# Attention and expert 0 taken in two halves of the batch, the first half ahead; the inverse deviation computed half by half on VectorE

## What is computed

```python
# step 1: autocorrelation attention
Q = layernorm(x) @ Wq + bq;  K = ctx[:, :56] @ Wk + bk;  V = ctx[:, :56] @ Wv + bv     # 16 heads of 8
corr = irfft(rfft(Q) * conj(rfft(K)))          # along the 56 positions
w, idx = top_k(corr.mean(-1), 4)               # 4 best shifts of each batch and head
out = sum_k softmax(w)_k * roll(V, -idx_k)
x = x + tanh(g_xattn) * (out @ Wo + bo)
# step 2: mixture of 8 experts, 2 per token
xf = layernorm(x)
weights = softmax over the two largest of (xf @ Wr + br)
x = x + tanh(g_ffn) * sum_e weights_e * (gelu(xf @ W1[e] + b1[e]) @ W2[e] + b2[e])     # hidden size 512
```

## Time and profile before

| | us |
|---|---|
| median of 3 executions (lowest, highest) | 133.50 (132.34, 134.25) |
| the profiled execution, its own time | 132.46 |
| its span, first to last instruction | 130.2 |
| mean granted clock of TensorE in it | 0.956 of full |
| PE busy | 117.5 (90%) |
| DVE busy | 89.9 (69%) |
| ACT busy | 80.5 (62%) |
| POOL busy | 62.9 (48%) |

### The profile page before, as it was taken

One profiled execution on the slowest core, in us unless ns is written; L12 is line 12 of the kernel. 1 busy time (PEld: TensorE's weight loads), 2 busy tenths in 40 slices (PEclk: granted clock), 3 DMA queues, 4 the chain that ended last, 5 costly groups with the idle time before them and its releaser, 6 DMA issues.

```text
span 130.2 us, 1685 instructions
## 1 busy us (share of the span) xinstructions
PE 117.5 (90%) x575; PEld 94.7 (73%) x575; DVE 89.9 (69%) x175; ACT 80.5 (62%) x107; POOL 62.9 (48%) x50
## 2 busy tenths in 40 slices
PE   6999969998878993959999999999999999999950
PEld 2397555544465891939999999999999999999930
DVE  1583687529386498999679877775775775775991
ACT  3027764401355755928878878878878878878900
POOL 0001460005203999999999999980330330330802
PEclk9999995559999999999999999999999999999998
DMA  3896000000310215400891340030040030000003
GB/s 93 234 406 249 0 0 5 3 0 0 101 60 0 82 79 161 162 6 9 238 337 43 107 146 0 0 141 0 0 141 3 5 141 0 0 0 0 0 0 141
DMA packets 3833, 10.07 MB, mean 77 GB/s; under 512 B 697, under 2 KB 1066, under 8 KB 3826
## 3 DMA queue, kind: packets, MB, share of 16 engines
q1 hardware_dynamic: 3154, 9.43, 21.5%
q10 hardware_dynamic: 672, 0.55, 1.5%
HBM read 9.49 MB, written 0.49 MB: 77 GB/s over the span
## 4 chain that ended last, share of the span: by engine, by line
PE 70%; DVE 14%; ACT 5%; issue 5%; POOL 2%; POOLq 1%; DVEq 0%
PE bank L772 23%; PE bank L799 22%; PE bank L641 7%; PE bank L658 3%; ACT prod L409 3%; POOL cf L329 2%; DVE hidl L617 2%; PE bank L664 2%; ACT hidh L416 2%; DVE prod L496 2%; DVE tw L496 2%; PE bank L718 2%; PE bank L735 1%; DVE qk L261 1%; PE bank L748 1%
## 5 line engine op out<-in xcount | busy, mean ns | idle before, releaser
L617 DVE TENSOR_TENSOR hidl<-prod,hidh 128x896 fp32r<-128x896 f32 (+1 forms) x34 | 45.3, 1339 | 19.8 <-ACT hidh L416 19.8
L409 ACT ACTIVATE prod<-bank,col_sb 128x896 f32<-128x896 f32 (+1 forms) x34 | 32.9, 967 | 14.5 <-PE bank L772 11.8
L323 POOL TENSOR_TENSOR wel<-we_sb,weh 128x512 fp32r<-128x512 f32 x16 | 25.6, 1604 | 20.9 <-issue 19.9
L416 ACT CAST hidh<-prod 128x896 fp32r<-128x896 f32 (+1 forms) x34 | 30.5, 899 | 1.0
L329 POOL TENSOR_TENSOR cf<-cf,kf 128x448 f32<-128x448 f32 x12 | 17.9, 1496 | 26.6 <-DVE kf L604 26.4
L799 PE MATMUL bank<-hidl,weh 128*128 128x448 f32 x64 | 18.5, 368 | 2.2 <-DVE hidl L617 2.2
L772 PE MATMUL bank<-xth,weh 128*128 128x448 f32 x64 | 18.6, 366 | 0.3 <-ACT xth L404 0.3
L772 PE MATMUL bank<-xtl,weh 128*128 128x448 f32 x64 | 18.6, 367 | 0.0
L772 PE MATMUL bank<-xth,wel 128*128 128x448 f32 x64 | 18.5, 365 | 0.0
L799 PE MATMUL bank<-hidh,weh 128*128 128x448 f32 x64 | 18.4, 367 | 0.0
L799 PE MATMUL bank<-hidh,wel 128*128 128x448 f32 x64 | 18.3, 365 | 0.0
(11 more groups left out here) (118 smaller groups left out, 116.7 us busy)
## 6 DMA issues: line engine op xcount, KB each, us to landing
we_sb<-in_w_experts SPq DMA_DIRECT2D x8, 512.0 KB, 5.0
route_b<-route_scratch SPq DMA_DIRECT2D x8, 448.0 KB, 3.6
out<-vf SPq DMA_DIRECT2D x2, 224.0 KB, 1.9
tb<-in_tab_b SPq DMA_DIRECT2D x1, 297.0 KB, 6.3
ta_c<-in_tab_ctx SPq DMA_DIRECT2D x1, 274.8 KB, 4.9
wa_sb<-in_w_attn SPq DMA_DIRECT2D x1, 256.0 KB, 5.7
x_sb<-in_x SPq DMA_DIRECT2D x1, 224.0 KB, 3.8
x_sb<-in_x ACTq DMA_DIRECT2D x1, 224.0 KB, 4.1
```

The costliest lines, as they stand in the source:

```text
L323: gp.tensor_tensor(wel[:, e, k, :], we_sb[:, e % RING, k, :], weh[:, e, k, :].bitcast(F32), ALU.subtract).then_inc(we_split, 1)
L409: act.activation(hid[:, n % 2, halves, :], bank[:, 2 * (n % 2):2 * (n % 2) + 2, 0:TOK][:, halves, :], ACT.Gelu, bias=col_sb[:, P_B1 + n:P_ ...
L416: act.copy(hidh[:, n % SLOTS, halves, :], hid[:, n % 2, halves, :]).then_inc(hid_hi, 1)
L617: ve.tensor_tensor(hidl[:, n % SLOTS, halves, :], hid[:, n % 2, halves, :], hidh[:, n % SLOTS, halves, :].bitcast(F32), ALU.subtract).then ...
```

## The change

- The attention, the second normalisation and expert 0 are done by half: the first half of the batch goes ahead on every engine, the second follows. Each step is a function of the half, and every engine has a list of calls in which first-half steps of a later stage stand ahead of second-half steps of an earlier one. Chunks 0 to 3 are four `hidden` and four `project` for the first half, then the same for the second.
- DVE's inverse deviation is computed per half: the chain of the kernel before, which was run once on 112 x 8 numbers per normalisation, is run twice on 112 x 4. (Both kernels use the seed and the refinement steps on DVE; neither takes a power on GpSimd.)
- The filler matmuls: 7 + 5 at the start instead of 13, none later.
- Logits and their differences take both halves at once, before hidl of chunk 1; DVE's chain of the routes is cut in two by one hidl.
- ACT rather than DVE copies the turned shift weights and both spectra of x, and `take_expert` (7, half) is followed by an addition that DVE does alone.
- POOL: the bias rows are loaded from its queue; xres in two parts, ahead of the centring matrix and only once both first normalisations are over; the rests of experts 0 and 1 in 16 pieces of 128 columns, as soon as ACT has made the rounded part; experts 2 to 7 only once the routes are computed (`route_ok`).
- SP loads experts 5 to 7 between the broadcasts of the routes instead of ahead of them.

```diff
         def _(sp):
-            for e in range(E - 1):
+            for e in range(RING + LEAD_BY_SCALAR):
                 load_expert(e)
...
             for e in range(E):
-                if e == ROUTES:
-                    load_expert(E - 1)
                 if e >= ROUTES:
                     sp.wait_ge(scaled_ok, 2 * (e - ROUTES + 1))
                 sp.dma_start(route_b[:, e % ROUTES, :, :], ...)
+                if e >= 1 and e + RING + LEAD_BY_SCALAR - 1 < E:
+                    load_expert(e + RING + LEAD_BY_SCALAR - 1)
         def _(gp):
+            gp.dma_start(rows_sb[:, :, :], bias_rows).then_inc(in_rows, 16)
+            def rest(e, k):
+                for at in range(0, H, PIECE):
+                    gp.tensor_tensor(wel[:, e, k, at:at + PIECE], ..., ALU.subtract).then_inc(we_split, 1)
...
+            gp.wait_ge(norm_ok, 2)
...
+            residual(0)
+            residual(1)
...
+            for e in range(LEAD_BY_SCALAR):
+                gp.wait_ge(in_we[e], 16)
                 for k in range(2):
...
+                    rest(e, k)
+            gp.wait_ge(route_ok, 1)
+            for e in range(LEAD_BY_SCALAR, E):
+                gp.wait_ge(in_we[e], 16)
+                for k in range(2):
+                    gp.tensor_copy(weh[:, e, k, :], we_sb[:, e % RING, k, :]).then_inc(lead_p, 1)
...
         def _(act):
+            chunk(0, HALF[0])
+            gelu(1, HALF[0])
+            normalise(x2, 1, 1)
+            lead_of_hidden(1, HALF[0])
+            gelu(2, HALF[0])
+            lead_of_tokens(1)
+            lead_of_hidden(2, HALF[0])
+            chunk(3, HALF[0])
+            chunk(0, HALF[1])
+            chunk(1, HALF[1])
+            act.wait_ge(ldif_ok, 1)
+            act.activation(ltanh[:, :, :], ldif[:, :, :], ACT.Tanh, scale=0.5).then_inc(ltanh_ok, 1)
+            chunk(2, HALF[1])
+            chunk(3, HALF[1])
         def _(ve):
+            def variances(times, half):
+                tiles = slice(half * HT, (half + 1) * HT)
...
+                link(ve.tensor_scalar(v, mv[:, tiles, 1], EPS, None, ALU.add))
+                link(ve.tensor_scalar(a.bitcast(I32), v.bitcast(I32), -0.5, GUESS, ALU.mult, ALU.add))
...
         def _(pe):
-            pe.wait_ge(warm_ok, 1)
-            keep_busy(FILL_START, 3)
...
-            keep_busy(FILL_TOP)
...
-            keep_busy(FILL_STEP)
...
-            keep_busy(FILL_NORM)
...
+            hidden(0, HALF[0])
+            hidden(1, HALF[0])
+            logits(1)
+            hidden(2, HALF[0])
+            project(0, HALF[0])
+            tokens_turned(1)
+            hidden(3, HALF[0])
+            project(1, HALF[0])
+            hidden(0, HALF[1])
...
+            hidden(4, BOTH)
+            project(2, HALF[1])
+            turn_routes()
+            hidden(5, BOTH)
+            project(3, HALF[1])
```

More of the change, by code:

```diff
@@ L433, in _ @@
+            chunk(2, HALF[1])
+            chunk(3, HALF[1])
+            for n in range(HC, LAST):
+                chunk(n, BOTH)
+            chunk(LAST, HALF[0])
+            chunk(LAST, HALF[1])
         @block.vector
@@ L492, in _ @@
[L492 to L500 removed]
+                    ve.wait_ge(x2_ok, half + 1)
+                    ve.wait_ge(x_spec, half + 1)
@@ L732, in _, with attention @@
                 mm.then_inc(y_mm, 1)
-            for half in range(2):
+            def attention(half):
                 pe.wait_ge(y_ok, half + 1)
@@ L803, in project @@
-                if n < E * HC - 1:
-                    mm.then_inc(y_expert, 1)
-            hidden(0)
-            hidden(1)
-            for n in range(E * HC):
-                if n + 2 < E * HC:
-                    hidden(n + 2)
-                if n == 3:
-                    turn_routes()
-                project(n)
+                for k, (w, t) in enumerate(operands):
+                    pe.wait_ge(hid_ok if k == 2 else hid_hi, unit(n, last))
+                    for half in range(halves.start, halves.stop):
+                        mm = pe.matmul(bank[:, 6 - 2 * (e % 2) + half, 0:TOK], w_of(w), t[:, slot, half, :],
+                                       start=(c == 0 and k == 0), stop=(c == HC - 1 and k == 2))
@@ new lines, in project @@
+                mm.then_inc(y_expert, 1)
+            pe.wait_ge(warm_ok, 1)
+            keep_busy(FILL_FIRST, 3)
+            pe.wait_ge(dc_ok, 1)
+            pe.wait_ge(in_rows, 16)
+            for half in range(2):
+                open_projection(0, 6, half)
+                open_projection(1, 4, half)
+            keep_busy(FILL_SECOND, 3)
+            context_spectra(0)
+            context_spectra(1)
+            x_spectra(0)
+            pe.wait_ge(in_wa, 16)
+            keys(0)
+            queries(0)
@@ new lines, in _ @@
+            x_spectra(1)
+            keys(1)
+            queries(1)
+            pe.wait_ge(in_tb, 16)
+            head_sums(0)
+            values(0)
+            correlations(0)
+            head_sums(1)
+            weights_turned(0)
+            correlations(1)
+            weight_spectra(0)
+            values(1)
+            repeated(0)
+            weights_turned(1)
+            add_residual(0)
+            weight_spectra(1)
+            output_products(0)
+            repeated(1)
+            attention(0)
```

591 lines of the change are left out of this document (310 added, 281 removed).

## The result

The changed kernel takes 138.17 us (median of 4 executions, 136.80 to 139.24), the kernel before 133.88 beside it (four executions here, 132.34 to 134.29). The ratio is 1.043 with a 95% interval of 1.031 to 1.054: slower, where I had forecast 131.8 us and no measurable change.

What follows compares the result with a forecast made beforehand. Time was taken as the routes' end, plus PE's unbroken expert matmuls behind it, plus whatever breaks that stretch: 49.0 + 73.0 + 7.5 = 129.5 us of span, with 2.26 around it 131.8; range for 8 in 10, 127.8 to 136.0.

Steps and rivals of the forecast that it cites:

- The routes at 49.0: End of the routes, after attention and expert 0: forecast at 49.0 us, between 48.0 and 53, 8.6 us earlier than before.
- I add 0.5 us for the clock and the bias rows: Allowance added to the routes' end of 48.5 us for a lower clock and for bias rows over POOL's queue.
- I get the first product at 13.9: Start of attention: DVE's first-half queries-times-keys product (prod) begins at 13.9 us, 0.3 earlier than before.
- the half clock: Rival: without fillers PE's clock stays at half from 18 us until expert 0 is under way; 138.8 us, chance 10%.
- "about seven" products: In the slow-clock rival: about seven 464- and 512-column products on the path, each 0.8 us more at half clock.
- before had ten us at half clock as well: Argument against the slow-clock rival: the kernel before also ran ten us at half clock, so only the excess counts.
- The halves themselves: Attention by halves: weights-times-values product (tw) at 23.4 us, 5.3 earlier; first gelu at 37.6, 5.6 earlier.
- the second: In attention: the second half's weights-times-values product starts at 27.3 us, after PE's first-half output products.
- The wait that takes the place of the gain: At the take of expert 2's output: DVE waits 8.0 us for POOL, PE stands still 5.3; 7.5 in all.
- the 1.2 that I took: After PE's idle stretch at expert 2: cost of the clock falling, taken as 1.2 us out of 0 to 3.4.
- Behind the routes, 73.0: From the routes to the end, without the new wait: 72.6 us before, 0.6 more for PE, 0.2 less at the end.
- Sum: Whole kernel: 49.0 + 73.0 + 7.5 = 129.5 us of span, with 2.26 around it 131.8 us.

Runs made afterwards that it cites:

- e3: Changed kernel with bias rows loaded from SP's queue and POOL's pairs started at the second normalisation instead of the routes: 133.42 us.
- e6: Changed kernel with all 13 starting fillers ahead of the wait for the bias rows, none behind (13 + 0): 135.90 us.
- e7: Changed kernel with 13 + 0 starting fillers, bias rows from SP's queue and 18 later fillers: 132.52 us, ratio 0.995 to the kernel before.
- e4: Changed kernel with 18 later fillers put into attention and ahead of expert 0: 134.13 us, ratio 1.022 to the kernel before.
- e13: e10 with DVE's first-half xtl ahead of the second half's inverse-deviation chain and 1 filler instead of 4 ahead of expert 0: 124.18 us, ratio 0.940.
- e8: e7 with POOL's additions placed in turns between its pairs: 126.71 us, ratio 0.935 to the kernel before.
- e11: Changed kernel with POOL's additions and pairs in turns, nothing else altered: 131.15 us.
- e9: Kernel before with POOL's pairs of experts 2 to 7 behind the routes and SP's loads of experts 5 to 7 between the broadcasts: 137.63 us, ratio 1.034.
- e10: e8 with five more fillers, 3 ahead of the head sums and 2 ahead of the correlations: 124.95 us, ratio 0.936.
- e1: Changed kernel with its bias rows loaded from SP's queue instead of POOL's: 137.48 us.
- e2: Changed kernel with POOL's pairs of experts 2 to 7 started at the second normalisation instead of at the routes: 134.83 us.

## Why the prediction was wrong, and where it was right

**The routes at 49.0: wrong by 6.6, and this is the step that failed.** "I add 0.5 us for the clock and the bias rows" stood for two terms, and both were mis-sized.

- *Start, "I get the first product at 13.9".* It came at 15.9. I priced the load at "nothing to 1 us" because 5 fillers stand behind it, and took those fillers for cover. They are the cost: PE has nothing left ahead of the wait, and does them after it, in 2.3 us (1.4 in e3). e6 gives 1.8 us back by order alone, e7 2.1. The queue of the load, about which I had argued, is 0.1 to 1.0, by the times at which PE could start on the rows.
- *The half clock.* e4 and e7 need 34.7 and 35.0 us from the first prod to the routes, the changed kernel 39.7: 4.7 to 5.0 us. It costs 1.25 between prod and tw, where steps of PE on the path are few (11.5 against 10.25 in e7), and 3.2 between the first gelu and the routes (13.9 against 10.7), where PE is dense. The rest, 0.3, lies between.

Between the changed kernel and e7 the two are 2.1 and 4.7, all of the 6.9 by which the routes differ (55.62 - 48.75). Taken one at a time, from e6 and from e4, they are 1.8 and 5.0.

I had this outcome as a rival, the half clock, at 138.8 us and 10%, deciding from routes after 53.4. Routes at 55.6 and 138.2 us are nearly its numbers, but in part by luck. It had the clock at half from 18 us until expert 0 without a break, for 5.5 us, and nothing for the start; the clock fell twice, with 10 us at full between, for 4.7, and the start added 2.0. The 5.5 was in the main "about seven" products at 0.8 each, which misreads the rows: 3.22 for four matmuls against 0.95 for two is 0.33 for one and 0.66 for a pair. I set the rival aside because "before had ten us at half clock as well". But those ten us were in the thin steps of attention, where the fall cost the changed kernel 1.25; its second fall is where the matmuls of expert 0 are, and costs 3.2. By the range, 127.8 to 136.0, the outcome had been left out.

**The halves themselves: right, once start and clock are what the steps assumed.** In e7, prod at 13.8 (13.9), tw at 24.0 (23.4), the second at 27.8 (27.3), xtl done at 37.5 (37.2), gelu at 38.1 (37.6), routes at 48.8 (48.5, to which I added the 0.5). The step from prod to tw was 0.75 longer than I had it and that from the first gelu to the routes 0.2 shorter (10.7 against 9.4 + 1.5). That xtl stands behind the second half's chain, and is late for it, e13 shows: 0.8 us, together with three fillers.

**The wait that takes the place of the gain: right, in place and size.** 8.10 against 8.0 for DVE and 5.17 against 5.3 for PE in the changed kernel. Counted from the routes, DVE comes to the take after 24.9 us (24.1) and POOL's addition ends after 32.9 (32.1): both 0.8 later, which cancels in the wait. Behind the routes there are 74.2 to 74.5 us in the halved kernels without the wait and 81.5 to 82.6 in those with the whole of it. e7 and e8, which differ in nothing else, are 7.7 apart, the half clock after the wait included; I had 7.5. e11 took 7.0 off the median, and e9 put the wait into the old kernel. Of that half clock the changed kernel had more than the 1.2 that I took: from 90.8 to about 96.6 us PE does dense matmuls at half, which is 2.9 us lost (an estimate, half of that stretch).

**Behind the routes, 73.0: 1.5 too small for e10, but not for the changed kernel's pace.** In e10 PE has 70.08 us of work there instead of 67.88. Six more matmuls are recorded (344 against 338), 1.2 us where I had counted 0.6, and an expert takes 9.9 instead of 9.7 us. Seven experts by 0.2 is 1.4, an estimate. For that pace I have no cause, and it is not the halves: 9.9 is seen in e9, the kernel before with the wait, and in e1, e7, e8 and e10 to e13; 9.7 in the changed kernel, e2, e3, e4 and e6.

**Sum.** 129.5 of span was forecast, 137.4 came: 6.6 at the routes and 1.3 behind them. As the changed kernel's pace was the 9.7 of the forecast, the 1.3 is, by the estimate above, in the main the longer half clock after the wait. What lies around the span was 1.8 instead of 2.26, and the median, 138.17, is 1.1 under the profiled execution.

## What to carry to other kernels

A filler counts only if it stands ahead of the wait that it covers; behind the wait it is paid for in full: 13 + 0 instead of 7 + 5 gave 1.8 us back. When idle time is removed by taking fillers out, look for the granted clock at the place where dense matmuls begin next, since there it cost the most here (3.2 of 4.7 us). And when an engine that works in order is held back for a good reason, look at the last thing in its queue, not the first: here the cure was to leave the wait and to move the additions between the pairs, which gave 7 us. With the start and the clock mended as well, the kernel went from 4% slower to 6% faster than before.
